# A recurrent block on one core: SyncE issues tokens first and decays two chunks ahead, and the last two chunks are turned early into other rooms

## What is computed

```python
xn = layernorm(x)
proj = xn @ in_proj_w.T                      # gate 4096 | x, B, C 6144 | dt 64
xBC = silu(conv1d(proj_xBC, 4 taps) + conv_bias)
dt_p = softplus(dt + dt_bias); dA = exp(dt_p * -exp(A_log))
state = state * dA_t + (dt_p * x)_t * B_t     # 64 heads, 64 x 128 each, over 1024 tokens
y_t = state @ C_t + D * x_t
s = (rmsnorm_by_group(y) * norm_weight * silu(gate)) @ out_proj_w.T
out = x + s * silu(xn @ W.T + bias + lora(xn))
```

## Time and profile before

| | before |
|---|---|
| three runs, us | 1748.84, 1750.83, 1754.08 (median 1750.83) |
| the profiled execution: its time, its span | 1753.88, 1752.1 |
| PE, DVE, POOL, ACT busy, share of the span | 97%, 81%, 68%, 63% |
| mean granted TensorE clock | 0.991 of full speed |
| moved by DMA | 304.78 MB, mean 174 GB/s |

### The profile page before, as it was taken

How to read it: one execution, slowest core, us unless ns; L and a number is a source line. 1 busy time by engine, 2 the same in 40 slices (tenths; PEclk the granted TensorE clock), 3 DMA queues, 4 the chain that set the end, 5 groups by cost and what they waited for, 6 DMA issues and landing times.

```text
span 1752.1 us, 31626 instructions
## 1 busy us (share of the span) xinstructions
PE 1697.6 (97%) x10792; PEld 1368.7 (78%) x10792; DVE 1420.8 (81%) x1840; ACT 1098.3 (63%) x2843; POOL 1190.4 (68%) x1255
## 2 busy tenths in 40 slices
PE   7988999999999999999998999999999999999986
PEld 5777888888888888888876888888888888888865
DVE  7868888887978888887876978888887878888885
ACT  4557576665757576665656667575666657576653
POOL 5428677675857767675786858678575857767564
PEclk9999999999999999999999999999999999999998
DMA  8545555555555555555787655565555565555555
GB/s 267 157 134 171 171 176 153 169 173 173 166 177 159 164 169 164 179 173 157 232 227 230 184 174 161 166 180 154 169 174 174 154 184 160 165 166 177 159 166 151
DMA packets 322416, 304.78 MB, mean 174 GB/s; under 512 B 88272, under 2 KB 255568, under 8 KB 322256
## 3 DMA queue, kind: packets, MB, share of 16 engines
q1 hardware_dynamic: 321216, 302.60, 58.0%
q10 hardware_dynamic: 1040, 0.16, 0.1%
HBM read 246.57 MB, written 56.10 MB: 173 GB/s over the span
## 4 chain that ended last, share of the span: by engine, by line
PE 80%; DMA 5%; DVE 5%; SPq 4%; issue 3%; ACT 2%; POOL 2%; ACTq 0%; POOLq 0%; DVEq 0%
PE ps_conv L1381 9%; PE ps_conv L1384 9%; PE ps_y L1544 7%; PE ps_conv L1387 6%; PE ps_out L1381 6%; PE ps_gate L1381 6%; PE ps_s L1565 6%; PE ps_out L1384 6%; PE ps_gate L1384 6%; PE ps_y L1549 5%; PE ps_out L1387 4%; PE ps_gate L1387 4%; DMA turned_d<-squares 3%; PE ps_conv L1388 2%; PE ps_g L1373 2%
## 5 line engine op out<-in xcount | busy, mean ns | idle before, releaser
L930 DVE SCALAR_TENSOR_TENSOR xc<-ps_conv,convw_sb,xc 128x511 f32<-128x511 f32 (+2 forms) x576 | 430.4, 747 | 96.7 <-ACT xc L694 83.1
L1288 POOL TENSOR_TENSOR cpre<-cpre,xc 128x1024 f32<-128x1024 f32 x112 | 268.5, 2397 | 52.8 <-ACT xc L700 29.9
L826 ACT ACTIVATE dtx<-x_tok,prefix_dt 128x64 f32<-128x64 f32 x1024 | 258.1, 339 | 72.1 <-DMA b_tok<-turned_d 72.0
L1321 POOL TENSOR_TENSOR square<-square 128x256 f32<-128x256 f32 x128 | 93.8, 733 | 305.6 <-ACT square L838 305.6
L1070 DVE TENSOR_TENSOR_SCAN decay<-decay,turned_x 128x512 f32<-128x512 f32 x250 | 290.4, 1203 | 9.2 <-DMA decay<-decays_d 9.0
L1381 PE MATMUL ps_conv<-xn_hi,wconv_hi 128*128 128x512 f32 x768 | 245.4, 441 | 0.0
L1384 PE MATMUL ps_conv<-xn_hi,wconv_lo 128*128 128x512 f32 x768 | 206.4, 390 | 0.0
L1381 PEld LDWEIGHTS ps_conv<-xn_hi,wconv_hi 128*128 128x128 f32 x768 | 144.4, 188 | 68.2 <-issue 43.6
L1544 PE MATMUL ps_y<-decay,dtx 128*64 128x128 f32 x1984 | 191.6, 280 | 2.7 <-ACT ps_y L808 2.7
L854 ACT ACTIVATE ynt_hi<-ps_y 128x512 fp32r<-128x512 f32 x126 | 75.2, 597 | 178.2 <-DVE ps_y L1128 175.1
L1549 PE MATMUL ps_y<-cpre,state 128*64 128x128 f32 x1760 | 172.1, 274 | 0.0
(11 more groups left out here) (236 smaller groups left out, 3783.0 us busy)
## 6 DMA issues: line engine op xcount, KB each, us to landing
decay<-decays_d SPq DMA_DIRECT2D x125, 512.0 KB, 5.1
cpre<-rows_d SPq DMA_DIRECT2D x112, 512.0 KB, 4.1
turned_d<-squares SPq DMA_DIRECT2D x512, 80.0 KB, 2.7
stage<-w_in_t SPq DMA_DIRECT2D x32, 1024.0 KB, 6.3
x_tok<-turned_d SPq DMA_DIRECT2D x128, 256.0 KB, 3.0
stage<-w_out_t SPq DMA_DIRECT2D x16, 1024.0 KB, 6.3
stage<-w_in_t SPq DMA_DIRECT2D x32, 256.0 KB, 3.9
b_tok<-turned_d SPq DMA_DIRECT2D x128, 64.0 KB, 2.9
```

The source lines that it names most:

```text
L826: scaled = e.activation(dtx[i % 2][:, h * HD:(h + 1) * HD].rearrange("p (a i) -> p a i", i=SQ), head_of(x_tok[i % 2], h), ACT.Copy, scale= ...
L930: e.scalar_tensor_tensor(acc[:, d:], ps[:, 0:BLK - d], convw_sb[:, tile, TAPS - 1 - d:TAPS - d], acc[:, d:], ALU.mult, ALU.add).then_inc(S ...
L1288: e.tensor_tensor(cpre[k % 2][:, :, :], cpre[k % 2][:, :, :], xc[i // CPB % 2][:, XT + 1, block_cols(i % NCH)].unsqueeze(1).to_broadcast([ ...
```

## The change

SP's step is reordered: the token round of chunk `i + 1` comes first, then the rows of chunk `i + 1`, then the decays of chunk `i + 2` (one chunk further ahead), and then all the rest: the decays of `AHEAD`, prefixes, normalized inputs, finished chunks and weights. In the prologue the decays of chunk 1 go ahead of the last rates' rows, and the last rates' sums (`rate_sums(3)`, with a wait for a round trip through DRAM) go behind the first token round of the loop.

Chunks 126 and 127 (`LATE`) get rooms of their own: DVE turns both at the end of step 124, right behind the mixing matrix of chunk 124, into the block of convolved values `xc0`, whose last chunk was 123 (`late_room`), and they have slots of their own in DRAM. SP's step 124 ends with both token rounds, one behind the other. Their readers take x and B from there (`x_tok_of`, `b_tok_of`, not shown). In steps 125 to 127 the mixing matrix moves to DVE's start of the step, ahead of the state and the gating of the chunk before, and on ACT the seed moves ahead of the square of the chunk before.

```diff
@@ -41,6 +41,7 @@
 AHEAD = (N - 1, N - 3, N - 2)
+LATE = (N - 2, N - 1)
@@ -169,7 +170,7 @@
-        turned_d = nc.dram_tensor("turned_d", [2, P, QUADS, TT * SQ], F32).ap()
+        turned_d = nc.dram_tensor("turned_d", [2 + len(LATE), P, QUADS, TT * SQ], F32).ap()
@@ -336,13 +337,33 @@
+        def late_room(part, i):
+            at = (2 * LATE.index(i) + part) * TT * P
+            return room[:, at:at + TT * P]
...
+        def turned_slot(i):
+            return 2 + LATE.index(i) if i in LATE else i % 2
@@ -396,6 +417,10 @@
                             ds[0:HEADS, :].rearrange("h (c i) -> h c i", i=P)).then_inc(st_rows[b, j], 16)
+
+            def rate_sums(q):
+                b, j = RATES[q]
+                first = j * CPB
                 w.wait_ge(S["pt"], q + 1)
...
@@ -413,6 +438,8 @@
                 if part == 5:
                     rate_totals(q)
+                    if q < len(RATES) - 1:
+                        rate_sums(q)
@@ -474,26 +501,28 @@
             def store_turned(i):
 
                 w.wait_ge(S["turned"], i + 1)
-                w.wait_ge(landed_tok[i % 2], 32 * (i // 2))
+                if i not in LATE:
+                    w.wait_ge(landed_tok[i % 2], 32 * (i // 2))
...
             def fetch_tokens(i):
 
                 w.wait_ge(S["st_turned"], 16 * QUADS * (i + 1))
-                if i >= 2:
+                if i >= 2 and i not in LATE:
                     w.wait_ge(S["dtx"], i - 1)
                     w.wait_ge(S["xw"], inner(i - 2))
                     w.wait_ge(S["mm_u"], inner(i - 2))
...
@@ -586,12 +615,20 @@
                 if s == 23:
                     store_turned(0)
                     fetch_tokens(0)
+                    fetch_decays(1)
             for i in range(N + DRAIN):
                 f = finished(i)
                 g, at = divmod(i, NCH)
                 left = BATCH * GROUPS - 1 - g
-                if i + 1 <= TAIL:
-                    fetch_decays(i + 1)
+                if i + 1 < LATE[0]:
+                    store_turned(i + 1)
+                    fetch_tokens(i + 1)
+                if i == 0:
+                    rate_sums(len(RATES) - 1)
+                if i + 1 < N and (i + 1) % NCH:
+                    fetch_rows(i + 1)
+                if i + 2 <= TAIL:
+                    fetch_decays(i + 2)
                 if i == TAIL - 6:
                     fetch_decays(AHEAD[0])
                 if i == TAIL - 2:
@@ -602,17 +639,12 @@
                     blk, r = divmod(i - TURN, CPB)
                     for c in ((0, 1), (2,), (3,), ())[r]:
                         fetch_normed(blk * CPB + c)
-                if i + 1 < N and (i + 1) % NCH:
-                    fetch_rows(i + 1)
                 if f is not None and f > NCH:
                     fetch_last(f)
                 if i > 0 and finished(i - 1) is not None:
                     store(finished(i - 1))
                 if f is not None and f <= NCH:
                     fetch_last(f)
-                if i + 1 < N:
-                    store_turned(i + 1)
-                    fetch_tokens(i + 1)
                 if i < N and left:
                     if at == 2:
                         fetch_gate(g + 1)
@@ -622,6 +654,10 @@
                         fetch_conv_x(g + 2)
                     if at == 7:
                         fetch_out(g + 1)
+                if i == TAIL:
+                    for late in LATE:
+                        store_turned(late)
+                        fetch_tokens(late)
             store(TOK - 1)
             w.wait_ge(S["stored"], 16 * TOK)
             for b, j in RATES:
@@ -824,10 +860,12 @@
                 if 0 <= m < N and conv_late(m) is not None:
                     silu(conv_late(m))
+                if TAIL < i < N:
+                    seed(i)
                 if 0 <= m < N:
                     w.wait_ge(S["mm_in"], m + 1)
...
@@ -858,7 +896,7 @@
                 for k in gated(i):
                     gate_silu(k)
-                if TAIL <= i < N:
+                if i == TAIL:
                     seed(i)
@@ -934,8 +972,13 @@
                 w.wait_ge(S["silu"], max(conv_no(nb, t) for t in range(TT)) + 1)
-                w.wait_ge(S["st_turned"], 16 * QUADS * i)
-                e.transpose(squares[:, :, :, :].rearrange("p b t i -> p t b i"),
+                if i in LATE:
+                    w.wait_ge(S["cpre"], later(TAIL - 1))
+                    w.wait_ge(S["skip"], TAIL)
+                    w.wait_ge(S["mm_g"], TAIL)
+                else:
+                    w.wait_ge(S["st_turned"], 16 * QUADS * i)
+                e.transpose(squares_of(i).rearrange("p b t i -> p t b i"),
@@ -1111,8 +1154,10 @@
                 if i < N:
                     if i <= TAIL:
                         last_factors(i)
-                    if i + 1 < N:
+                    if i + 1 < LATE[0]:
                         turn(i + 1)
+                if TAIL < i < N:
+                    mixing_matrix(i)
@@ -1126,8 +1171,6 @@
                     w.wait_ge(S["square"], m + 1)
                     w.wait_ge(S["sgate"], m // CPB * CPB + CPB)
                     e.tensor_tensor(turns(y_bank(m)), turns(y_bank(m)), gate_of(m), ALU.mult).then_inc(S["yg"], 1)
-                if TAIL < i < N:
-                    mixing_matrix(i)
                 if u >= 0:
                     acc, scale = out_sum[:, u % NCH, :], rstd_col[:, u % 2:u % 2 + 1]
                     if u < N - 1:
@@ -1167,6 +1210,9 @@
                     fin(f, u + 1)
                 if i <= TAIL:
                     mixing_matrix(i)
+                if i == TAIL:
+                    for late in LATE:
+                        turn(late)
                 if i < N and conv_early(i) is not None:
                     taps(conv_early(i))
                 if i == TAIL - 4:
```

30 lines of the change are left out of this document (20 added, 10 removed).

## The result

| | before | changed |
|---|---|---|
| median of the runs (lowest to highest), us | 1751.94 (1748.84 to 1754.08) | 1816.11 (1815.96 to 1816.91) |
| ratio, 95% interval | | 1.0366 [1.0352, 1.0381] |
| span of the profiled execution, us | 1752.1 | 1814.2 |
| PE busy, us; mean granted clock | 1697.6; 0.991 | 1717.8; 0.975 |

What follows compares the result with a forecast made beforehand. PE was taken as the bound from 150 to 850 us, standing still in three places. Terms 34 (ring) + 9 (late decays) + 0 (chunks 125 to 127) - 1 (start) = +42 us gave 1793 us, range 1768 to 1811.

Steps and rivals of the forecast that it cites:

- the ring: Finished chunks f = 0 to 7: SP, ACT and DVE wait on each other in a closed loop; +34 us (+19 to +50).
- the tail: Last chunks: late decays of chunks 125 and 126, +9 us, and products of chunks 125 to 127, 0.
- What bounds the kernel: PE is full from 150 to 850 us; it idles 11.1 us at 850 to 1000, 18.6 at the end, 5.17 in step 2.
- The steady part: Steps at 150 to 850 us: SP's queue has room and PE covers later rows; nothing gained or lost.
- first `x_again` out: Step 58: SP issues `x_again` of f = 0 at 859.8 us, where it went at 849.23.
- landing inside the closed links: In the loop behind chunks 58, 60, 61, 62 and 64, `x_again` lands 4.9 us after issue, 7.5 under load.
- sum of seven steps: From `x_again` of f = 0 to f = 7: five closed links 80.5, two open 19.4, seven rests 33.5; 133.4 us.
- PE's slack: At chunk 65's output product PE has 2.1 us of slack, subtracted from the 36.6 us by which the SiLU is late.
- The late decays: Step 122: decays of chunks 125 and 126 land late, DVE stands still 8.8 us; +9 us (+6 to +12).
- Chunks 125 to 127: Last three products: early tokens remove the token wait but other waits come in; 0 us (-8 to +4).
- The start: First steps: chunk 1's tokens come some 6 us sooner, its rows later; -1 us (-5.2 to +1).
- Rival 3: Heavier: all landings at 7.5 us (+16) and PE at half clock behind seven gaps (+7); 1816 us, chance 0.12.

Runs made afterwards that it cites:

- e15: Kernel before with SP's new order in steps 57 to 67 alone; 1798.34 us, ratio 1.0265.
- e14: Kernel before up to step 111, the whole change from step 112 on; 1768.84 us, ratio 1.0096.
- e9: Kernel before with decays of chunk 1 before the loop and, in step 0, rows of chunk 1, token round, then totals; 1746.54 us, ratio 0.9970.
- e6: Changed kernel with the rows of chunk 1 issued ahead of the token round of step 0; 1810.31 us, ratio 1.0341.
- e13: Kernel before with e9's start and the change's SP order in steps 1 to 56 and 68 to 111 alone; 1755.43 us, ratio 1.0014.
- e1: Changed kernel with store, factor and addend of the first batch's finished chunks issued ahead of the token round; 1776.01 us, ratio 1.0139.
- e8: Changed kernel with prefixes and normalized inputs issued behind factor and addend in steps 57 to 64; 1807.17 us, ratio 1.0322.
- e10: Kernel before with only store, factor and addend of the first batch's finished chunks issued behind the token round; 1757.89 us, ratio 1.0034.
- e17: Changed kernel with factor and addend of the first batch's finished chunks issued by ACT instead of SP; 1774.77 us, ratio 1.0126.
- e16: e9 with factor and addend of the first batch's finished chunks issued by ACT instead of SP; 1743.74 us, ratio 0.9957.
- e5: Changed kernel with ACT's SiLU of the first batch's factors moved behind the next step's last convolution tap; 1795.89 us, ratio 1.0253.
- e11: Changed kernel with the repairs of e1, e2 and e6, plus chunk 8's store and chunks 8 and 9's factor and addend ahead of the round; 1761.73 us.
- e2: Changed kernel with the early decays of chunks 125 to 127 issued ahead of their step's token round; 1809.15 us, ratio 1.0327.
- e4: Kernel before with only the early turns of the last two chunks, and seed and matrix first; 1753.05 us, ratio 1.0015.

## Why the prediction was right and wrong

By the single parts, the change costs +46.2 (e15) + 16.7 (e14) + 0.5 (e9, e6) = +63.4 us of the 64.2 measured, where the prediction has +34, +9 and -1. The forecast failed by the size of two terms, the ring (12 us too small) and the tail (8 us by e14's median, 4 us by the offsets within the traces).

- **What bounds the kernel: right.** All of the loss lies at the three places named. PE's idle time at 850 to 1050 us was forecast at about 45 us and is 42.9.
- **The steady part at nothing: right** (699.46 of 700 us busy; e13 up to chunk 67).
- **The ring, +34: mechanism right, size too small by 12 us.** e1, e8, e10 and e17 show it four ways, and e15 that it is all in steps 57 to 67. Its terms against the trace:

| step of the prediction | forecast | measured |
|---|---|---|
| first `x_again` out | 859.8 | 863.0 (2.5 of it because the turned tiles came that much later) |
| SiLU to the turn's end | 6.5 | 6.5 (four of five), 5.2 |
| store to fetch | 3.5 | 3.2, once 3.9 |
| fetch to `x_again` | 6.0 | 3.3 to 9.3, mean 6.0 over all seven, 6.4 over the closed five |
| landing inside the closed links | 4.9 | 4.5 to 6.8, mean 5.8 |
| last landing | 4.9 | 7.6 |
| sum of seven steps | 133.4 | 138.3 |
| PE's slack | 2.1 | none |

 The step that failed is the choice of the landing. I took 4.9 us, from three issues of the tail, where at most the rows of one chunk and the factor go out right ahead of `x_again`, for transfers that go out right behind rows, decays and inputs; the row that belonged to such a place (7.5 us) was kept for the upper bound alone. It isn't the traffic of the stretch that makes the difference: there, too, `x_again` lands in 4.3 us when only store and factor go out right ahead of it (e10, 210 GB/s). With five closed links (5.8 instead of 4.9) and the last landing (7.6), this choice is 7 of the 13 us by which the ring was too small. The 2.6 us that the prediction set against its rows were further off still: no median landing of `x_again` here is under 4.2 us (e17). The second is the slack. I subtracted it from one pair of rows. The runs show none: ACT's last SiLU of the batch and chunk 66 are late by the same amount, within 1.6 us, in all eight kernels:

| | e16 | e17 | e1 | e10 | e5 | e8 | e15 | changed |
|---|---|---|---|---|---|---|---|---|
| SiLU of f = 7 later than before, us | -8.7 | 0.3 | 6.4 | 10.0 | 25.0 | 36.4 | 46.5 | 47.4 |
| `ynt_lo` of chunk 66 later, us | -8.7 | 1.0 | 7.1 | 9.4 | 24.4 | 37.8 | 47.9 | 49.0 |

- **The late decays, +9: right, a little small.** DVE's wait was 10.4 us instead of 8.8, and 11.2 us went through (e14). The 1.6 us are the landing again: SP issued the decays at 1725.7, which is the forecast 1675.4 and the 50 us of the ring, and DVE's scan began 6.5 us later, not 4.9; 4.9 was a row of 256 KB transfers, and these are 512 KB each.
- **Chunks 125 to 127 at nothing: right in the sum.** Their last product began 32.0 us behind that of chunk 124 (31.5 forecast, 31.4 before), that of 125 11.8 us behind it (11.6), that of 126 25.0 (23.0). What I missed is a second small ring in step 122 (`x_again` of chunk 8), 3 us (e11). It hides behind the late decays: e2, without these, gets back 7.0 us and not 11.
- **The start, -1: about right (+0.5)**, by two effects of 5 to 6 us each that cancel; that they do is luck, and +0.5 can't be told from -1. The late rows were named, but bounded at +1; had they been repaired the start would have gained 5.3.
- **Rival 3 has the right number, 1816, by luck, and half of the right cause.** Landings were longer than 4.9 us, if not 7.5. Its clock part isn't on the path of the ring: PE's busy time grew by 20.2 us for the same work (clock 0.85 against 0.98 from 850 to 1000 us), and still chunk 66 follows ACT's SiLU within 2 us in the table above. PE was slow in time that it would otherwise have waited.

So the sum would have been 34 + 4.9 (steps) + 3.2 (first issue) + 2.7 (last landing) + 2.1 (slack) = 46.9 for the ring. The range failed otherwise: the ring's 46.2 lies within its own bounds (+19 to +50), but the upper end of 1811 lets the ring alone rise and leaves the tail at +9 and the start at -1, and these two came to 9 us more.

The early turns of the last two chunks aren't what costs (e4: +2.8), and what helps is in the change only in part: **e16**, the kernel before with the change's start (decays of chunk 1 before the loop, totals last) but rows first, and with factor and addend issued by ACT, takes 1743.7 us against 1752.6 of before beside it, 0.9957 [0.9943, 0.9970].

## What to carry to other kernels

Before moving a transfer in an in-order queue, follow it all the way round: who waits for it, what stands behind that engine's wait, and whether the queue itself waits for that further up. If so, every transfer between the queue's own wait and the moved one is a link of a loop, and it is paid once per step. Here the loop was opened by issuing the transfer ahead of the queue's wait (e1) or from another queue (e17); moving the waiting instruction within its engine closed it elsewhere and gave back only 20 us (e5). And a landing time is to be read from a row in which as much is issued right ahead of the transfer as will be there, not where the row is cleanest.

## What the runs showed of the hardware

A tiny DVE instruction was held up to the end of POOL's beside it. DVE's `last` (128x16) took 550 ns on the mean from 150 to 850 us before and 894 ns in the changed kernel, as its groups by line show (first before, then after):

```profile
L1081 DVE TENSOR_TENSOR last<-decay,prefix_dt 128x16 f32<-128x16 f32 x49 | 27.0, 550 | 0.5
```

```profile
L1124 DVE TENSOR_TENSOR last<-decay,prefix_dt 128x16 f32<-128x16 f32 x48 | 42.9, 894 | 0.5
```

The timeline of the changed kernel shows why. With POOL's `cpre` under way `last` ends when that ends, 2.27 us; with POOL idle it takes 0.18:

```profile
360.42 2.37 POOL L1334 TENSOR_TENSOR cpre<-cpre,xc 128x1024 f32<-128x1024 f32 x1 [4.06 <-DMA cpre<-rows_d]
360.56 2.27 DVE L1124 TENSOR_TENSOR last<-decay,prefix_dt 128x16 f32<-128x16 f32 x1
...
372.06 0.18 DVE L1124 TENSOR_TENSOR last<-decay,prefix_dt 128x16 f32<-128x16 f32 x1
```

All 19 `last` of that stretch that no POOL instruction overlaps took 0.17 to 0.18 us, and the 29 others 0.24 to 2.38. It is the later rows that move `cpre` onto `last`: in the seven kernels that issue the rows ahead of the round in the steady steps (before, e4, e9, e10, e14 to e16) the mean is 536 to 556 ns, in the twelve that issue them behind it 852 to 1039 ns. The scan of the decays, whose second input is a PSUM bank, isn't held up: 21 scans of the kernel before lie wholly inside a `cpre` and took 1.19 to 1.22 us like the others. The Trainium skill ("SBUF — State Buffer", Who interferes with whom) says that a DVE instruction with two SBUF inputs contends with a GpSimd instruction that reads SBUF, and that this contention is an exclusive lock; these rows agree. It cost nothing here, since PE covers it. Executions also differ by up to 3.8 us from the first steps on: chunk 2 came 0.7 to 3.8 us later than in the trace of before in four kernels whose start is the same (e4, e10, e14, e15), which is why the terms above are taken from offsets within one trace where that was possible.
